# Two graph layers on one core: item rows in one-chunk groups mostly from SyncE, a quarter of their copies on VectorE, x and the weights loaded later, another order between the layers

## The reference, cut to what matters

```python
# layer 0
h = item @ W_item.T + b_item
x = layernorm(x + relu(adj @ h + (x @ W_user.T + b_user)))
# layer 1
Wh = x @ W
e = leaky_relu(Wh @ a[:128] + (Wh @ a[128:]).T, 0.2)
att = softmax(where(adj > 0, e, -9e15), axis=1)
out = layernorm(x + elu(att @ Wh))
```

## Time and profile before

| | |
|---|---|
| median of three timed runs | 2785.01 us (2784.74 to 2786.03) |
| profiled execution | 2787.46 us, its span 2785.7 us |
| TensorE busy | 2742.5 us, 98% of the span |
| VectorE busy | 2420.5 us, 87% |
| ScalarE busy | 890.2 us, 32% |
| layer 1 | 46.7 to 1412.3 us |
| layer 2 | 1426.5 us to the end |

### The profile page before, as it was taken

One profiled execution on the slowest core, in us unless ns is written; L12 is line 12 of the kernel. 1 busy time (PEld: TensorE's weight loads), 2 busy tenths in 40 slices (PEclk: granted clock), 3 DMA queues, 4 the chain that ended last, 5 costly groups with the idle time before them and its releaser, 6 DMA issues.

```text
span 2785.7 us, 22633 instructions
## 1 busy us (share of the span) xinstructions
PE 2742.5 (98%) x6953; PEld 1276.6 (46%) x6953; DVE 2420.5 (87%) x2559; ACT 890.2 (32%) x678; POOL 3.5 (0%) x33
## 2 busy tenths in 40 slices
PE   7999999999999999999989999999999999999998
PEld 5444444444444444444544444444444444444454
DVE  4888888888888888888889898989898989898987
ACT  4555555555555555555550000001010101010111
POOL 0000000000000000000000000000000000000000
PEclk9999999999999999999999999999999999999999
DMA  9999999999999999999880000000000101010000
GB/s 283 326 315 319 304 316 320 310 317 314 309 314 319 312 309 317 314 317 322 252 215 0 19 16 19 15 20 21 14 29 5 34 0 34 0 34 0 15 8 14
DMA packets 331972, 468.18 MB, mean 168 GB/s; under 512 B 57624, under 2 KB 165384, under 8 KB 331784
## 3 DMA queue, kind: packets, MB, share of 16 engines
q1 hardware_dynamic: 197848, 239.32, 29.7%
q10 hardware_dynamic: 134064, 228.15, 26.8%
HBM read 443.85 MB, written 23.55 MB: 168 GB/s over the span
## 4 chain that ended last, share of the span: by engine, by line
PE 97%; DVE 1%; DMA 1%; ACT 0%; issue 0%; SPq 0%; ACTq 0%; DVEq 0%
PE bank L542 47%; PE bank L581 24%; PE bank L582 23%; PE bank L540 1%; PE bank L518 1%; PE bank L569 1%; DVE adj_t L618 1%; PE bank L481 0%; DMA b_item_row<-in_L_gnn_b_item_dram 0%; PE bank L472 0%; DMA s_scratch<-ts_row 0%; DMA area_r<-s_scratch 0%; ACT area_p L974 0%; DVE area_h L717 0%; ACTq L293 0%
## 5 line engine op out<-in xcount | busy, mean ns | idle before, releaser
L542 PE MATMUL bank<-adj_t,area_h 128*128 128x512 f32 (+1 forms) x3160 | 1337.0, 583 | 4.9 <-DVE adj_t L618 4.9
L881 DVE SCALAR_TENSOR_TENSOR adj_t<-area_r,c_col,area_h 128x1024 f32<-128x1024 uint8 (+2 forms) x790 | 957.5, 1254 | 122.3 <-PE bank L582 121.0
L618 DVE STREAM_TRANSPOSE adj_t<-area_r 128x2048 f32<-128x2048 f32 (+3 forms) x400 | 892.3, 2231 | 176.9 <-PE bank L542 90.2
L542 PEld LDWEIGHTS bank<-adj_t,area_h 128*128 128x128 f32 x3160 | 598.0, 190 | 718.9 <-issue 711.3
L984 ACT ACTIVATE mask_out<-adj_t 128x4096 uint8<-128x4096 f32 (+1 forms) x200 | 699.9, 3501 | 649.9 <-DVE packing L692 384.2
L581 PE MATMUL bank<-adj_t,area_r 128*128 128x512 f32 x1580 | 808.4, 593 | 8.2 <-DVE adj_t L881 8.2
L582 PE MATMUL bank<-adj_t,area_r 128*128 128x512 f32 (+1 forms) x1580 | 776.1, 573 | 0.0
L582 PEld LDWEIGHTS bank<-adj_t,area_r 128*128 128x128 f32 x1580 | 300.6, 190 | 378.7 <-issue 378.7
L581 PEld LDWEIGHTS bank<-adj_t,area_r 128*128 128x128 f32 x1580 | 299.9, 190 | 350.9 <-issue 324.1
L811 DVE TENSOR_TENSOR area_h<-area_p,bit_of 128x2048 uint32<-128x2048 uint32 (+1 forms) x100 | 220.7, 2207 | 0.0
L1104 ACT ACTIVATE area_h<-bank,empty_sums 128x512 f32<-128x512 f32 x10 | 6.9, 687 | 474.4 <-PE bank L582 474.4
(11 more groups left out here) (115 smaller groups left out, 431.3 us busy)
## 6 DMA issues: line engine op xcount, KB each, us to landing
area_r<-in_adj_dram SPq DMA_DIRECT2D x312, 512.0 KB, 10.3
area_r<-in_adj_dram ACTq DMA_DIRECT2D x312, 512.0 KB, 10.8
area_r<-in_adj_dram SPq DMA_DIRECT2D x78, 480.0 KB, 8.9
area_r<-in_adj_dram ACTq DMA_DIRECT2D x78, 480.0 KB, 8.7
mask_scratch<-packed ACTq DMA_DIRECT2D x40, 320.0 KB, 9.7
area_p<-mask_scratch SPq DMA_DIRECT2D x20, 640.0 KB, 6.2
x_scratch<-area_s ACTq DMA_DIRECT2D x20, 256.0 KB, 8.8
area_h<-x_scratch SPq DMA_DIRECT2D x10, 512.0 KB, 4.0
```

The source lines that it names most:

```text
L542: mm = nc.tensor.matmul(acc1[par][:, 0:live], h[:, c * SPC + s, :], adj_t[:, c % 2, s * width:s * width + live], start=(c == 0 and s == 0) ...
L618: nc.vector.transpose(dst, src).then_inc(half_turned, 1)
L881: nc.vector.scalar_tensor_tensor(out=prob[:, n, 0:width], in0=lhs, scalar=c_col[:, b:b + 1], in1=unpacked[:, c % 2, n, 0:width // 4].bitca ...
```

## The change

- Items: seven groups, the first three of one chunk each, then three pairs and chunk 9. ScalarE loads its quarters only for groups 0 to 3 (chunks 0 to 4), and makes a small copy, which brings its table load, after group 0. SyncE loads all four quarters from group 4 on.
- TensorE's first wait is for w_item alone; VectorE waits for b_item.
- VectorE copies the second bank of each odd chunk (turned_rows), ScalarE the rest. TensorE's waits follow with upper_turned_sb.
- ScalarE issues unit c // 2 of the adjacency after its copy of each odd chunk c, so units 0 to 4 at c = 1 to 9. SyncE issues units 0 to 4 straight after the items, then the weights; x after unit 6.
- In block 0 the x product is at chunk 9, its transpose at chunk 8, and the weight products and copies two or three chunks later (one for the last copy).
- Between the layers: t_blocks are loaded ahead of load_right(0), for 32 steps and not 64; f_row is loaded by ScalarE after chunk 7 of block NB; the first chunk's unpack is cut in two halves, one beside z_rows, one after the columns; the normed rows, the remaining packs and the sums come after the weights of layer 2's first chunk.

```diff
-    ITEM_GROUPS = [(0,)] + [(c, c + 1) for c in range(1, NC - 1, 2)] + [(NC - 1,)]
+    ITEM_GROUPS = [(0,), (1,), (2,)] + [(c, c + 1) for c in range(3, NC - 1, 2)] + [(NC - 1,)]
+    ACT_GROUPS = 4
...
@@ -311,13 +314,13 @@
         @block.sync
         def _(sp):
             sp.dma_start(w_in[:, 0, :], w_item).then_inc(w_item_loaded, 16)
-            for group in range(2):
-                load_items(sp, group, (0, 1))
-            sp.dma_start(b_item_row[:, :], b_item.rearrange("(a d) -> a d", a=1).to_broadcast([P, D])).then_inc(w_item_loaded, 16)
+            load_items(sp, 0, (0, 1))
+            load_items(sp, 1, (0, 1))
+            sp.dma_start(b_item_row[:, :], b_item.rearrange("(a d) -> a d", a=1).to_broadcast([P, D])).then_inc(b_item_loaded, 16)
             for group in range(2, len(ITEM_GROUPS)):
-                load_items(sp, group, (0, 1))
-            load_adjacency(sp, 0, 0, IB, (0, 1))
-            load_adjacency(sp, 0, 1, IB, (0, 1))
+                load_items(sp, group, (0, 1) if group < ACT_GROUPS else range(A))
+            for u in range(RAW):
+                load_adjacency(sp, 0, u, IB, (0, 1))
...
-            load_x(0, IB)
-            for u in range(2, RAW):
-                load_adjacency(sp, 0, u, IB, (0, 1))
-
             def block_loads(k, par, width, first):
                 for u in range(UPB):
                     if first and u < RAW:
                         continue
-                    if u == 0:
+                    if u == (RAW + 2 if first else 0):
...
+                for lo in ((0,) if part == 0 else (Q, 2 * Q)):
+                    n = min(STEPS, lo + Q) - lo
+                    for a in range(A):
+                        src = t_dram[:, BASE[a] + lo * Q:BASE[a] + (lo + n) * Q].rearrange("o (s j) -> (o s) j", j=Q)
+                        sp.dma_start(t_blocks[a * Q:a * Q + n, lo:lo + Q], src).then_inc(t_loaded[part], 16)
...
+
+            sp.wait_ge(t_stored_dram, 16 * (NB - 2))
+            load_t(0)
             sp.wait_ge(x1_stored_dram, 16 * NB)
             sp.wait_ge(half_turned, last + 2 * 6)
             load_right(0)
-            sp.wait_ge(t_stored_dram, 16 * NB)
-            sp.wait_ge(s_stored_dram, 16 * NB)
-            load_t(0)
             sp.wait_ge(half_turned, last + 2 * 8)
-            sp.dma_start(f_row[:, 0:SB], s_dram[:, 0:SB].to_broadcast([P, SB])).then_inc(s_loaded[0], 16)
...
+                    pe.wait_ge(upper_turned_sb, (c - 1) // 2)
...
+                pe.wait_ge(upper_turned_sb, (c + 1) // 2)
...
-            pe.wait_ge(w_item_loaded, 32)
+            pe.wait_ge(w_item_loaded, 16)
...
-                if c == 1:
+                if c == 4:
...
-                if c == 4:
+                if c == 6:
...
-                if c == 6:
+                if c == 8:
...
-                    if c == 4:
+                    if c == (9 if first else 4):
...
+            def turned_rows(c, q):
+                n = steps_of(c)
+                m = min(4, n - 4 * q)
+                turned = item_t[:, c % 2, 0:n * P].rearrange("p (q s) -> p s q" if n == SPC else "p (s q) -> p s q", s=n)
+                return turned[:, 4 * q:4 * q + m, :], item_banks[c % 2][q][:, 0:m * P].rearrange("p (s q) -> p s q", s=m)
+
+            dve.wait_ge(b_item_loaded, 16)
             for c in range(NC):
+                if c + 1 < NC and c % 2 == 0:
+                    dve.wait_ge(item_turned, c + 2)
+                    if c >= 1:
+                        dve.wait_ge(h_product, c)
+                    nc.vector.tensor_copy(*turned_rows(c + 1, 1)).then_inc(upper_turned_sb, 1)
...
-                    if first and c == 3:
+                    if first and c == 6:
...
-                    if first and c == 6:
+                    if first and c == 8:
...
-                    if first and c == 8:
+                    if first and c == 9:
...
-                    if c == 2:
+                    if c == (8 if first else 2):
...
-            residual(NB, TAIL)
-            pack2(NB, NC - 2, TW)
-            pack3(NB, NC - 2, TW)
-            row_stats1(NB, TAIL)
-            scores(NB, TAIL)
-            dve.wait_ge(t_max_taken, NB + 1)
-            nc.vector.reduce_max(t_part[:, :], t_max[:, :], AX_X).then_inc(top_partial, 1)
-            pack1(NB, NC - 1, TW)
-            dve.wait_ge(top_turned, 1)
-            nc.vector.reduce_max(t_top[:, :], ps_top[0:1, 0:P], AX_X).then_inc(top_found, 1)
-            pack2(NB, NC - 1, TW)
-            dve.wait_ge(t_loaded[0], 16 * A)
-            nc.vector.transpose(t_cols[:, 0:S1], t_blocks[:, 0:S1]).then_inc(t_cols_made, 1)
-            dve.wait_ge(top_broadcast, 1)
-            top = ps_top[:, P:P + 1]
-            nc.vector.tensor_scalar(shift[:, 2:3], top, -1.0, F_CAP / (1.0 - SLOPE), ALU.mult, ALU.add)
-            nc.vector.tensor_scalar(shift[:, 0:1], top, -1.0, None, ALU.mult)
-            nc.vector.tensor_scalar(shift[:, 1:2], top, 1.0 - SLOPE, None, ALU.mult).then_inc(shifts_made, 1)
...
-            normed(NB, TAIL)
-            pack3(NB, NC - 1, TW)
-            summed(NB, TAIL)
-
-            def unpack(k, par, width, c):
+            def unpack(k, par, width, c, steps=None):
...
+                lo, hi = steps or (0, steps_of(c))
+                n = hi - lo
...
+                done = nc.vector.tensor_tensor(unpacked[:, c % 2, lo:hi, 0:w], packed_in[:, par, c, None, 0:w].to_broadcast([P, n, w]),
+                                               bit_of[:, lo:hi, None].to_broadcast([P, n, w]), ALU.bitwise_and)
+                if hi == steps_of(c):
+                    done.then_inc(mask_unpacked, 1)
...
+            residual(NB, TAIL)
+            unpack(0, 0, SB, 0, (0, SPC // 2))
+            row_stats1(NB, TAIL)
+            scores(NB, TAIL)
+            dve.wait_ge(t_max_taken, NB + 1)
+            nc.vector.reduce_max(t_part[:, :], t_max[:, :], AX_X).then_inc(top_partial, 1)
+            dve.wait_ge(t_loaded[0], 16 * A)
+            nc.vector.transpose(t_cols[:, 0:Q], t_blocks[:, 0:Q]).then_inc(t_cols_made, 1)
+            dve.wait_ge(top_turned, 1)
+            nc.vector.reduce_max(t_top[:, :], ps_top[0:1, 0:P], AX_X).then_inc(top_found, 1)
...
+            dve.wait_ge(shifts_made, 1)
+            capped(0)
+            dve.wait_ge(constants_made, 9)
+            ab_columns(0)
+            unpack(0, 0, SB, 0, (SPC // 2, SPC))
...
-                    unpack(0, 0, SB, 0)
                     dve.wait_ge(mask_made, NC * (NB + 1))
...
-                    if first and c == 8:
+                    if first and c == Q // SPC:
...
+                    if first and c == 0:
+
+                        normed(NB, TAIL)
+                        pack2(NB, NC - 2, TW)
+                        pack3(NB, NC - 2, TW)
+                        pack1(NB, NC - 1, TW)
+                        pack2(NB, NC - 1, TW)
+                        pack3(NB, NC - 1, TW)
+                        summed(NB, TAIL)
+                    if first and c == 1:
+                        dve.wait_ge(t_loaded[1], 16 * 2 * A)
+                        nc.vector.transpose(t_cols[:, Q:3 * Q], t_blocks[:, Q:3 * Q]).then_inc(t_cols_made, 1)
                     if first and c == 2:
-                        dve.wait_ge(t_loaded[1], 16 * A)
-                        nc.vector.transpose(t_cols[:, S1:S1 + Q], t_blocks[:, S1:S1 + Q]).then_inc(t_cols_made, 1)
-                    if first and c == 4:
...
-            for group in range(len(ITEM_GROUPS)):
+            load_items(act, 0, (2, 3))
+            act.wait_ge(constants_made, 1)
+            nc.scalar.copy(table_warm[:, 0:1], ones[:, 0:1])
+            for group in range(1, ACT_GROUPS):
                 load_items(act, group, (2, 3))
             for c in range(NC):
                 act.wait_ge(item_turned, c + 1)
-                if c == 1:
-                    load_adjacency(act, 0, 0, IB, (2, 3))
-                if c == 3:
-                    load_adjacency(act, 0, 1, IB, (2, 3))
                 if c >= 2:
                     act.wait_ge(h_product, c - 1)
                 n = steps_of(c)
                 turned = item_t[:, c % 2, 0:n * P].rearrange("p (q s) -> p s q" if n == SPC else "p (s q) -> p s q", s=n)
-                for q in range(-(-n // 4)):
+                for q in range(1 if c % 2 == 1 else 2):
                     m = min(4, n - 4 * q)
                     last = nc.scalar.copy(turned[:, 4 * q:4 * q + m, :], item_banks[c % 2][q][:, 0:m * P].rearrange("p (s q) -> p s q", s=m))
                 last.then_inc(item_turned_sb, 1)
-            for u in range(2, RAW):
-                load_adjacency(act, 0, u, IB, (2, 3))
+                if c % 2 == 1:
+                    load_adjacency(act, 0, c // 2, IB, (2, 3))
...
+                    if isinstance(k, int) and k == NB and c == 7:
+                        act.wait_ge(half_turned, k * HALVES + 2 * 8)
+                        act.wait_ge(s_stored_dram, 16 * (NB - 2))
```

(40 more changed lines are left out.)

16 lines of the change are left out of this document (3 added, 13 removed).

## The result

The changed kernel takes 2805.18 us (median; 2801.17 to 2810.91) beside 2785.36 for the kernel before: ratio 1.0071, 95% interval 1.006 to 1.0082. It is 20 us slower where 7 faster was forecast. The profiled execution took 2805.18, its span 2803.4. First the page after: part 4, the chain by engine (before, 97% TensorE), and of part 5 the group of the adjacency product (L538 now): busy, mean ns, idle time before it and its releaser.

The account below looks back on a forecast made before the run. TensorE, 97% of the chain, was taken to bound the kernel, so only its waits could give time. Terms 2.8 - 0.5 + 4.7 = 7.0 us, off 2785.01, gave 2778.0 us; range 2772.0 to 2784.5.

Parts of the forecast that it names:

- the three places: TensorE's waits before its first item transposes, the first adjacency product (4.0 us) and layer 2's first product (8.22 us).
- The two signs that it named for being wrong: Block 0's chunks 1 to 7 wait over 3 us for adjacency, or TensorE starves for items and stays at lower clock.
- Term 1a: Setup: when the work would let layer 1 start; item transposes 7.5 us earlier, VectorE's copy costing 0.7, start 39.9 us.
- Term 1b: Setup: when adjacency data lets layer 1 start; unit 1 lands at 41.5, start 43.9 us, 2.8 gained.
- the sentence on the floor: Setup: with the tail as it is, layer 1 could start at 46.7 - 7.5 + 0.7 = 39.9 us.
- Term 1c: Block 0, loads behind units 0 and 1: x, then unit 7 landing at 81 to 86 us; 0.5 us lost.
- Term 2: Between the layers: earlier capping and a split unpack gain 4.7 us, 14.2 us becoming 9.5.
- The clock: TensorE's slow first products in layers 1 and 2 stay as they are, give or take 1.5 us.
- the rival with ScalarE standing still: Setup: ScalarE's adjacency issues block, 22.2 us in all; layer 1 starts at 62.1, time 2795.7 us; chance 0.05.
- Unit 7 is late: Rival, block 0: data at its upper bound, start 46.7, 1.5 us lost later, time 2781.8 us; chance 0.24.
- The data is in time: Rival, setup: adjacency lands in time, so work bounds layer 1's start at 39.9; time 2773.5 us; chance 0.20.
- the forecast's own mechanism: Setup: SyncE's added item packets, sharing turns with ScalarE's queue, delay adjacency units 0 and 1 by 9.0 to 11.2 us.

Follow-up runs that it names:

- e12: e3 with the rows of x of every block issued by GpSimd on its own queue: 2778.84 us, ratio 0.997.
- e3: The changed kernel with ScalarE again loading its two quarters of every item group, as before the change: 2798.62 us, ratio 1.0037.
- e11: The changed kernel with the rows of x of every block issued by GpSimd on its own queue: 2793.18 us, ratio 1.0024.
- e4: The changed kernel with x behind unit 8 in SyncE's queue, ahead of unit 9: 2810.82 us, ratio 1.0073.
- e1: The kernel before with only the changed order between the layers: 2782.34 us beside 2787.64, ratio 0.9982.
- e5: The changed kernel with all loads of the setup in their old order and split: 2790.66 us, ratio 1.0019.
- e6: e3 with block 0's x loaded as 128 packets of 2 KB, same bytes and place, outputs differ: 2791.84 us, ratio 1.0013.
- e8: The kernel before with TensorE's first wait for w_item alone and VectorE waiting for b_item: 2786.82 us, ratio 1.0004.
- e9: e5 with the rows of x of every block issued by GpSimd on its own queue: 2778.07 us, ratio 0.9967.
- e10: The kernel before with the edits of e1 and e8 and the rows of x issued by GpSimd: 2778.37 us, ratio 0.9969.

## Why the prediction was wrong

**The path.** Right: only the stages around the three places count; nothing in the loops changed. The two signs that it named for being wrong are what the profile shows: stops in chunks 1 to 7, and starving for items, though with the lower clock only behind the last of these waits (1.00 to 39.1 us, then 0.72 to 45.2).

**Term 1a** held where the data let it: with the items on both queues the start is 42.7 to 43.1 (e12, e3), for a floor of 39.9. The 2.8 to 3.2 us more go largely to waits in the item stage (in e3 1.9 for items and 1.7 for ScalarE's first copy). VectorE's copy was priced at 0.65 from its bias addition of the same size and takes 1.08; it lay in idle time and cost nothing on the path.

**Term 1b is the first failed step.** Unit 1 was put at 41.5 and was complete at 51.0. Three sizes make up the 9.5 us, by the packets' records and the units' semaphores. First the base: 33.1 was read for SyncE's part, but both queues' transfers of a unit count on one semaphore and the view gives their landings in the order of issue; SyncE's last packet of unit 1 ended at 35.9, and the unit was complete at 36.5. Then the last 4 KB packet of SyncE's ends at 28.3 where it ended at 20.5: 7.8 us, priced at 4.9 to 7.1. From there to the last 512 B item packet it is 9.8 where it was 2.5: 7.3 us, priced at 4.1, since the 54 packets in half a microsecond were taken for the rate, and from 23 to 39 us SyncE's queue had 1302 in 16, 81 a microsecond and not 108. Units 0 and 1 behind them take 12.9 for 13.5, so 36.5 + 7.8 + 7.3 - 0.6 = 51.0. And the 41.5 chosen lay under the lower end of the term's own sum, 42.1, for a reason that had no size.

The term also held adjacency alone to be at stake. It missed that the items themselves, in the same queue, would starve TensorE: 9.3 us in five waits, where the sentence on the floor let it go at its own pace. Its last item product ends at 45.15 for 42.66 before. Before, the start came 4.03 us behind that end; so by the items alone it would have come at about 49.2 (an estimate from these rows), later than before and outside the term's bounds, and adjacency adds the other 4.3.

**Term 1c is the second.** Unit 7 was put at 81 to 86 and 0.5 us lost; it was complete at 103.3. Two of its sizes failed. Units 2 to 6 were put behind unit 1 at 5.7 us each, to 70. But from unit 5 on a unit goes to a slot that VectorE must first have emptied in block 0. e12 starts at 42.7, 1.2 before the forecast, with no x in SyncE's queue: its unit 6 is complete at 76.3 and its unit 7 at 81.7, wanted at 84.6 by the forecast's own reckoning: 2.9 us were left for x. And x was priced at "3 us alone and several times that beside another queue", 5 to 10 us, with no row for the second. In the changed kernel its packets take 9.9 us (81.8 to 91.7), and unit 7 is 11.0 later than in e11 (103.3 for 92.3). With the start where it was forecast, in e3, they take 18.6, and unit 7 is 16.6 later than in e12 (98.3 for 81.7): a stop of 12.5 us. In the whole x costs 13.4 (after against e11). For the items the prediction used the rule of its rows, 96 packets against 95. For x that rule, at the 81 packets a microsecond above, gives 25 us, near the upper end of what the runs have, 9.9 to 27.3 (e4), and far outside 5 to 10. What sets x's pace within these is not shown.

**Term 2** was right. The timeline after, between the layers (the counterparts are the earlier trace rows):

```profile
1435.11 1.22 DVE L783 TENSOR_TENSOR area_h<-area_p,bit_of 128x1024 uint32<-128x1024 uint32 x1
...
1440.12 0.15 DVE L802 TENSOR_SCALAR shift<-bank 128x1 f32<-128x1 f32 x1
...
1440.30 0.75 DVE L807 TENSOR_SCALAR area_r<-area_r,shift 128x1024 f32<-128x1024 f32 x1
...
1443.87 2.04 PE L577 MATMUL bank<-adj_t,area_r 128*128 128x512 f32 x2 [3.62 <-DVE adj_t L886]
```

The capping follows the shift at once, half of the unpack stands beside z_rows, and from 1434.19 to the first product are 9.7 us for 14.2 (forecast: 9.5). Alone it measured 5.3 (e1).

**The clock** was left as it was, give or take 1.5 us. At the start it gave back about that (1.4 us in the first 64 products, after 8.3 us of idling for 4.0). But the stop before chunk 6, which the forecast didn't have, cost 2.7 us more at the lower level. A stop's price is its length and what the clock then takes, and the second does not follow from the first: 0.1 us for 16 products after 1.96 us, 2.7 after 6.86, but 2.1 after 12.52 (e3).

**The rivals.** ScalarE's issues were short, 0.82 to 1.76 us a pair behind each odd chunk; the rival with ScalarE standing still did not happen, though its time, 2795.7, was the nearest: that would have been luck. The issues that stood were SyncE's: 10 of adjacency in 34.2 us, one of them 5.93. "Unit 7 is late" came true with a price of 1.5, for 8.8 us of stops in block 0 and 2.7 of clock. "The data is in time" fell. What was missing is the forecast's own mechanism at its true size: 11.2 us, from stretches of half to four microseconds, was taken for a bound where the runs have 15.1, and no rival began where it is passed.

The Trainium skill, "DMA: Bandwidth & Descriptors", section "Queues, rings and completion order", says that an engine drains a whole packet, typically 9 to 17 descriptors, before it turns to the next queue. Of the turns the trace after agrees, as far as equal counts can tell (1302 packets against 1304). Of their size no run here tells: what the profile records as a packet is a single row of 128 B, 512 B or 2 KB on these two queues, and equal counts would come out as well if an engine took several rows of each in a turn.

## What to carry to other kernels

Where two queues are busy, count packets, not bytes: a transfer of many short rows delays all that stands behind it in its queue, at worst by about its packet count times the other queue's packet time (here 25 us; x's packets took 9.9 to 27.3), and it is cheap only where the other queue is empty (3.4), which any shift in time can undo. So put what is wanted first on both queues in the same order, and give loads of short rows to a queue on which nothing urgent stands behind them (here GpSimd's: 2778 for 2786.5 us, faster than both kernels). An earlier start is worth what the next shortage leaves of it: follow each load to its user a block further before counting it, with the buffers that it must wait for. And where two queues count on one semaphore, don't read from the order of the counts which of them landed.

## What the runs showed of the hardware

- Two queues can share packet for packet over 16 us too: 1302 packets with 1.23 MB against 1304 with 2.51; with 128 B rows over 6 us 573 with 0.14 MB against 578 with 1.12. With 128 B rows this is not the rule: 1500 against 782 in 8 us (e3), 2034 against 759 (after).
- x's 2048 packets of block 0 in SyncE's queue took 3.4 us with ScalarE's queue empty (before), and beside it 9.9 (after), 17.9 (e5), 18.6 (e3) and 27.3 (e4).
- One of these queues alone moved 200 GB/s with 2 KB packets (52 to 60 us), both together 371.
- SyncE's issues of x stood for 21 us in sum while its queue was full (e3); GpSimd's four took 2.7.
- GpSimd's queue is recorded with 128 packets for 2048 rows of 128 B. Whether that, its being a third queue or the earlier issue helps is open; for block 0 fewer packets were enough (e6).
- VectorE's copy of 128 x 512 from PSUM in the order of turned_rows takes 1.08 us; a bias addition of the same size takes 0.65.
- Why e5 and e8 scatter over 15 us is not shown. With x's packets out of SyncE's queue it falls to under 2 us (e9, e10).
